# One copy for two carries, the conv gate moved to the head of its slot, and end states scaled on GpSimd

## The chip, the cores and the metric

The kernel runs on one core of one Trainium2 chip. The core has five engines that run their own instruction streams and wait for one another through semaphores: TensorE (PE), VectorE (DVE), ScalarE (ACT), GpSimd (POOL) and SyncE (SP), which issues most transfers here. The metric is the device time in microseconds (us), the median of the runs shown. A trace comes from one profiled execution.

## The reference

A layer in two parts, on x of shape (8, 1024, 256), all in fp32. The first is a selective state-space block, cut here to what matters:

```python
xn = x * rsqrt(mean(x*x) + 1e-6) * norm_w
x_branch, gate = split(xn @ W_in.T)                    # 512 + 512 channels
xc = silu(causal_conv4(x_branch) + conv_b)
dt = soft_clamp(softplus(xc @ W_dt.T + b_dt), 0.001, 0.1, 0.5)
Bp, Cp = xc @ W_B.T, xc @ W_C.T                        # 16 states
dA = exp(soft_clamp(dt[..., None] * A, -8, 8, 0.5))
def step(h, t):
    h = h * dA_t + dB_t * x_t[:, :, None]
    nrm = sqrt(sum(h*h, axis=(1, 2)))                  # over 512 channels x 16 states
    fac = minimum(20.0 / (nrm + 1e-8), 1.0)
    h = where(t % 10 == 0, h * fac, h)
    return h, einsum('bdn,bn->bd', h, C_t) + D_param * x_t
x = layernorm(x + x + scale * ((y * silu(gate)) @ W_out.T))
```

So the state runs freely for ten steps, and then it is scaled down if its norm is above 20. The second part is a mixture of experts (8 experts, top 2) with another layernorm; the change does not touch it.

## The kernel before

`ssm_phase` is the first part and `moe_phase` the second; only the first is changed. The sequence is cut into 52 blocks of 20 steps for all 8 batches. The outer loop over `i` is a pass; a pass has 16 slots `s`. A slot belongs to quarter `q = 4*i + s//4` and to batch `u = s % 4` of that quarter: a quarter is ten time steps of four of the eight batches, one slot is ten steps of one batch. In each slot VectorE runs one `tensor_tensor_scan` (L479) over 128 partitions x 704 elements: 4 channel groups x 16 states x 11 positions, the first of the 11 being the carry, the state with which the ten steps begin. Its factor comes from `DA` (where that first position is 0) and its addend from a PSUM tile `DBX`, one of two halves. In even slots `mult` (L454) writes ten of the 11 positions of two halves and `carry` (L469, or the memset of L464 for the first two quarters) the first one: it takes the last position of the end states `H` of the same four batches, two quarters back, times the factor `FC`. So there are 16 carries of 64 elements in a pass, with a step of 11 elements on either side.

The factor is made once per quarter. ScalarE squares the end states into `SQ` (L285), TensorE sums them over partitions with the constant matrix `ONE` (L703, 1/400), VectorE reduces them to four sums `SN` in slots with u = 2 (`norm_sum`, L485), GpSimd takes the power -0.5 (L631) and bounds it (L633). Behind that, in the same GpSimd slot, it multiplies the states of one batch by C (L640); TensorE then adds up the 16 states with an identity matrix (`y_sum`, L658 and L662).

Each pass also prepares later blocks, two or three ahead, in fixed slots. The queues are in program order, so that order is written out by hand:

- ScalarE: squares of x (L398) in slot 15, `RST` (L294) and `XB` (L301) in slot 1, exponentials of `DA` (L275, 128x2560 elements) in slots 1, 3, 5 and 15, the conv tanh `TB` (L312) in slot 5 behind the exponential, table-changing functions in slot 12, and 64 tanh of `DA` (L383) spread over the slots by the list `DUE`.
- TensorE: the sum of the squares of x (L713) and the projections (L668) in slot 0, conv in slots 2 and 3, the dt products (L687) in slots 6 and 7, which need `XC`.
- VectorE: `XC` (L528) in slot 6 behind that slot's multiplications, carries, `norm_sum` and scan; `dt_x` (L442), the product of dt and x, in slots 0 and 4; `SG` (L557) in slot 15.
- GpSimd: `XN` (L623), the normalized x, in slot 15; it is the input of the next pass's projections.

Of the kernel before, what the change touches and what calls it, by code (L numbers as in the profile page):

```python
# [8 lines left out]
ALU = mybir.AluOpType  # L9
# [9 lines left out]
NQ = 2 * NC  # L19
# [3 lines left out]
def ok(j):  # L23
    return 0 <= j < NB


def ssm_phase(nc, d, YA, X2d, LGd, Bd, Cd):
    ctx = ExitStack()
    with ctx:
# [15 lines left out]
        ID = sb("ID", [128, 128])  # L45
        ONE = sb("ONE", [128, 128])
        MEAN = sb("MEAN", [128, 128])
# [31 lines left out]
        HALF = sb("HALF", [128, 4])  # L79
        FC = sb("FC", [128, 2, 4])  # L80
        PM = ctx.enter_context(nc.psum_tensor("PM", [128, 2048], F32))
        PA = ctx.enter_context(nc.psum_tensor("PA", [128, 512], F32))
# [16 lines left out]
        s_halo, s_sgh, s_dx, s_dxh, s_hc = sem("halo"), sem("sgh"), sem("dx"), sem("dxh"), sem("hc")  # L99
        s_min, s_dt, s_xn, s_pow, s_fac = sem("min"), sem("dt"), sem("xn"), sem("pow"), sem("fac")  # L100
        s_ve, s_sd, s_x2 = sem("ve"), sem("sd"), sem("x2")
# [9 lines left out]

        PRE_C, PRE_CV, PRE_W, N_PRE = 10, 28, 30, 35
        loads = [
# [145 lines left out]
        def scalar_program(eng):  # L259
# [8 lines left out]

            DUE = [0, 0, 3, 8, 13, 15, 18, 26, 34, 36, 41, 48, 55, 55, 55, 59, 64]

# [6 lines left out]
            for i in range(-4, NB + 3):  # L277
                for s in range(16):
                    q = 4 * i + s // 4
                    if s % 4 == 0 and 1 <= q <= NQ - 2:  # L280

                        eng.wait_ge(s_scan, 4 * q)
                        if q >= 2:
                            eng.wait_ge(s_nrm, q - 1)
                        eng.activation(SQ[:], H[:, (q - 1) % 3].rearrange(  # L285
                            "p u (a t) -> p u a t", t=11)[:, :, :, 10], ACT.Square).then_inc(s_hsq, 1)
                    if s == 1 and ok(i + 3):
                        j = i + 3
                        eng.wait_ge(s_ssum, j + 1)
                        if ok(i + 2):  # L290
                            eng.wait_ge(s_br, 2 * j - 1)
                        if j > 0:
                            eng.wait_ge(s_xn, j)
                        eng.activation(RST[:], PA[:, 320:480], ACT.Copy).then_inc(s_ms, 1)  # L294
                    if s == 1 and ok(i + 2):
                        j = i + 2
                        for m, p in enumerate((PA, PZ)):
                            eng.wait_ge(s_br, 2 * j + m + 1)
                            if m == 0 and j > 0:
# [3 lines left out]
                                           ACT.Copy).then_inc(s_xb, 1)  # L303
                    if s in (1, 3, 5) and ok(i):
                        exp_a(i, (s + 1) // 2)
                    if s == 5 and ok(i + 2):
                        j = i + 2
                        for n, (p, m) in enumerate(((PZ, 1), (PA, 0))):
                            eng.wait_ge(s_cv, 2 * j + n + 1)
                            if n == 0 and ok(i + 3):  # L310
                                eng.wait_ge(s_ssum, j + 2)
                            eng.activation(TB[:, 2 * m:2 * m + 2].rearrange("p a b t -> p (a b t)"), p[:, 0:320],  # L312
                                           ACT.Tanh).then_inc(s_th, 1)
                    if s == 9 and ok(i + 2):
                        j = i + 2
# [71 lines left out]
                    if s == 15 and ok(i + 1):  # L387
                        eng.wait_ge(s_z64, 64 * (i + 2))
                        exp_a(i + 1, 0)
                    if s == 15 and ok(i + 4):  # L390

                        j = i + 4
                        eng.wait_ge(s_xt[j % 2], one(j))
                        if ok(i + 1):
                            eng.wait_ge(s_sg, 2 * (i + 2))
                        elif ok(i + 2):
                            eng.wait_ge(s_xc, 2 * (i + 3))
                        eng.activation(TB[:, 0:2].rearrange("p a b t -> p a (b t)"), XT[:, j % 2],  # L398
                                       ACT.Square).then_inc(s_sq, 1)
            lg_out(eng, NB - 1)  # L400
            eng.wait_ge(s_lgd, lg_done(NB))

        def vector_program(eng):
            eng.memset(ONE[:], 1.0 / 400).then_inc(s_pre, 1)
            eng.memset(MEAN[:], 1.0 / 256).then_inc(s_pre, 1)
# [10 lines left out]
            eng.tensor_scalar(PV[:, 0, :], PV[:, 0, :], 0.5, None, ALU.mult).then_inc(s_pre, 1)  # L416
            eng.wait_ge(s_pre, 12)
            for k in range(4):
# [40 lines left out]
            def carry(q, u):  # L459
                o = DBX(u).rearrange("p (a t) -> p a t", t=11)[:, :, 0]  # L460
                if 4 * q + u >= 2:
                    eng.wait_ge(s_scan, 4 * q + u - 1)
                if q < 2:
                    eng.memset(o, 0.0).then_inc(s_ca, 1)  # L464
                else:
                    h = H[:, (q - 2) % 3, u].rearrange("p (a t) -> p a t", t=11)[:, :, 10]
                    if u == 0:
                        eng.wait_ge(s_fac, q - 1)
                    eng.tensor_scalar(o, h, FC[:, q % 2, u:u + 1], None, ALU.mult).then_inc(s_ca, 1)  # L469

            def scan(q, u):
                eng.wait_ge(s_m1, 4 * q + u + 1)
                eng.wait_ge(s_ca, 4 * q + u + 1)
                if u == 0:
# [26 lines left out]
            for i in range(-4, NB + 3):  # L501
                live = ok(i)
                for s in range(16):
# [4 lines left out]
                    if live and s == 4:  # L508
                        dt_x(2 * i + 1)
                    if live and u % 2 == 0:  # L510
                        mult(q, u)
                        mult(q, u + 1)
                        carry(q, u)
                        carry(q, u + 1)
                    if u == 2 and 1 <= q <= NQ - 2:
                        norm_sum(q - 1)
                    if live:
                        scan(q, u)
                    if u == 0 and 0 <= q - 3 < NQ:
                        z_out(q - 3)  # L520
                    if s == 6 and ok(i + 2):
                        j = i + 2
                        for n, (p, m) in enumerate(((PZ, 1), (PA, 0))):
                            eng.wait_ge(s_th, 2 * j + n + 1)
                            if n == 0 and j >= 2:
# [4 lines left out]
                                TB[:, 2 * m:2 * m + 2].rearrange("p a b t -> p (a b t)"), 1.0, p[:, 0:320],  # L530
                                ALU.add, ALU.mult).then_inc(s_xc, 1)
                    if s == 13 and ok(i - 1):
                        j = i - 1
# [34 lines left out]
        def gpsimd_program(eng):  # L568
            eng.wait_ge(s_pre, PRE_CV)
            for i in range(-4, NB + 3):  # L570
                live = ok(i)
                for s in range(16):
# [52 lines left out]
                    if u == 2 and 1 <= q <= NQ - 2:  # L625

                        p = q - 1
                        eng.wait_ge(s_red, p + 1)
                        if p >= 2:
                            eng.wait_ge(s_ca, 4 * (p + 1))  # L630
                        eng.tensor_tensor(FC[:, p % 2], SN[:, p % 2], HALF[:], ALU.pow).then_inc(s_pow, 1)  # L631
                        eng.wait_ge(s_pow, p + 1)
                        eng.tensor_scalar(FC[:, p % 2], FC[:, p % 2], 1.0, 0.0, ALU.min, ALU.max).then_inc(s_fac, 1)  # L633
                    if live:
# [7 lines left out]
        def tensor_program(eng):  # L642
# [49 lines left out]
            for i in range(-4, NB + 3):  # L692
                if i == 0:
                    eng.wait_ge(s_pre, N_PRE)
                for s in range(16):
# [4 lines left out]
                    if u == 0 and 1 <= q <= NQ - 2:  # L700
                        p = q - 1
                        eng.wait_ge(s_hsq, q)
                        eng.matmul(NP(p), ONE[:], SQ[:], start=True, stop=True).then_inc(s_nrm, 1)  # L703
                    if u == 2:
# [556 lines left out]
```

## Time and profile before

| | us |
|---|---|
| median of 3 runs (3082.57 to 3089.11) | 3087.56 |
| the profiled execution, its own time | 3084.8 |
| its span, first to last instruction | 3082.6 |

| engine | busy us | share of the span |
|---|---|---|
| TensorE, matmuls | 2659.4 | 86% |
| VectorE | 2550.2 | 83% |
| ScalarE | 2268.4 | 74% |
| GpSimd | 1993.6 | 65% |

The shares are means over two phases. VectorE is over 90% busy from the second of forty slices of the span to the 33rd and below 40% behind that. The scans start at 77.29 us, the last starts near 2562 and the second phase begins near 2589. A record of VectorE or ScalarE lasts a little longer than the distance to the start of the next one, since the end of one instruction overlaps the start of the next; the time that an instruction occupies is read from start to start. In a timeline the number in brackets is the idle time of the engine ahead of the instruction, with what ended it.

### The profile page before, as it was taken

The page shows a single profiled execution, that of the slowest core. Times are in us where ns is not written, and L with a number is a line of the kernel's source. Part 1 is how long each engine was busy: PE and PEld are TensorE (multiplying, and loading weights), DVE is VectorE, ACT ScalarE, POOL GpSimd, SP SyncE. Part 2 cuts the span into 40 slices and gives each one's busy share as a digit, 9 for nine tenths or more (in the row PEclk, how much of TensorE's full clock was granted, in tenths as well). Part 3 has the DMA queues.
Part 4 walks back from the last instruction along what each step waited for, and adds up shares of the span by engine and source line. Part 5 has one row for each costly group of instructions (what it writes and reads, how often), then busy time and mean ns, then how long its engine had stood idle before and what let it go on. Part 6 is the DMA issues. An engine that isn't in the chain of part 4 may idle for free. (4 is left out here: it accounts for less than half of the span.)

```text
span 3082.6 us, 51144 instructions
## 1 busy us (share of the span) xinstructions
PE 2659.4 (86%) x16400; PEld 2420.8 (79%) x16400; DVE 2550.2 (83%) x3869; ACT 2268.4 (74%) x5161; POOL 1993.6 (65%) x2033
## 2 busy tenths in 40 slices
PE   4899898988989889998899998998999874899992
PEld 4888888888888888888888888888888873667662
DVE  1999999999999999999999999999999996321123
ACT  6888888888888888888888888888888860211113
POOL 0676777777777777777777777777777672443325
PEclk8999999999999999999999999999999986899996
DMA  2122222222222222222222222222222222133226
GB/s 66 57 70 70 71 62 76 70 70 73 66 70 69 70 74 65 72 77 64 72 70 70 70 68 76 68 72 74 63 73 66 69 69 91 31 96 73 73 46 228
DMA packets 153972, 225.69 MB, mean 73 GB/s; under 512 B 46056, under 2 KB 92776, under 8 KB 152552
## 3 DMA queue, kind: packets, MB, share of 16 engines
q1 hardware_dynamic: 131208, 188.98, 21.3%
q0 software_dynamic: 9216, 12.59, 2.3%
q10 hardware_dynamic: 13280, 20.86, 2.0%
q8 instruction: 130, 2.13, 0.3%
q14 instruction: 138, 1.13, 0.1%
HBM read 189.26 MB, written 33.05 MB: 72 GB/s over the span
## 5 line engine op out<-in xcount | busy, mean ns | idle before, releaser
L640 POOL TENSOR_TENSOR H<-H,CB 128x640 f32<-128x640 f32 x832 | 1242.4, 1493 | 499.8 <-DVE H L479 496.6
L479 DVE TENSOR_TENSOR_SCAN H<-DA,PM 128x704 f32<-128x704 f32 x832 | 1322.4, 1605 | 2.5 <-ACT DA L275 2.0
L383 ACT ACTIVATE DA<-DT,SM 128x160 f32<-128x160 f32 x3328 | 1111.7, 430 | 1.3
L662 PE MATMUL YB<-H,ID 128*128 128x160 f32 x6656 | 1052.6, 310 | 0.1
L662 PEld LDWEIGHTS YB<-H,ID 128*128 128x128 f32 x6656 | 991.6, 192 | 16.5 <-issue 11.2
L454 DVE TENSOR_TENSOR PM<-PM,BB 128x640 f32<-128x640 f32 x832 | 640.7, 814 | 5.1 <-issue 0.4
L275 ACT ACTIVATE DA<-DA 128x2560 f32<-128x2560 f32 x208 | 485.4, 2334 | 1.6
L687 PE MATMUL PA<-XC,WDT 128*128 128x160 f32 x832 | 168.3, 371 | 146.9 <-DVE XC L528 146.9
L687 PEld LDWEIGHTS PA<-XC,WDT 128*128 128x128 f32 x832 | 155.2, 246 | 162.5 <-DVE XC L528 162.5
L631 POOL TENSOR_TENSOR FC<-SN,HALF 128x4 f32<-128x4 f32 x206 | 210.5, 1022 | 94.5 <-DVE SN L485 90.5
L1117 POOL DMA_INDIRECT YA<-YS,IG x48 | 75.3, 1569 | 239.6 <-ACT YS L940 228.1
L469 DVE TENSOR_SCALAR PM<-H,FC 128x64 f32<-128x64 f32 x824 | 229.2, 322 | 0.0
L703 PE MATMUL YB<-SQ,ONE 128*128 128x256 f32 x412 | 129.3, 396 | 99.3 <-ACT SQ L285 99.3
L761 PE MATMUL PZ<-WO,Z 128*80 128x256 f32 x832 | 189.8, 381 | 0.1
L1173 PE MATMUL PE<-XTE,W 128*128 128x384 f32 x512 | 169.0, 491 | 10.1 <-issue 9.2
L1183 PE MATMUL PE<-W,HT 128*128 128x256 f32 x768 | 167.7, 380 | 6.1 <-issue 6.1
L1183 PEld LDWEIGHTS PE<-W,HT 128*128 128x128 f32 x768 | 145.3, 190 | 30.2 <-issue 10.7
L761 PEld LDWEIGHTS PZ<-WO,Z 128*80 128x80 f32 x832 | 125.8, 151 | 50.0 <-issue 1.2
L1173 PEld LDWEIGHTS PE<-XTE,W 128*128 128x128 f32 x512 | 97.6, 192 | 78.6 <-issue 13.7
L485 DVE TENSOR_REDUCE SN<-YB 128x4 f32<-128x256 f32 x206 | 85.5, 415 | 85.6 <-PE YB L703 85.6
L703 PEld LDWEIGHTS YB<-SQ,ONE 128*128 128x128 f32 x412 | 65.8, 190 | 112.8 <-ACT SQ L285 112.8
L934 ACT ACTIVATE HT<-PE,B 128x384 f32<-128x384 f32 x64 | 37.1, 582 | 158.0 <-PE PE L1173 155.5
(164 smaller groups left out, 3636.4 us busy)
## 6 DMA issues: line engine op xcount, KB each, us to landing
BB<-Bd SPq DMA_DIRECT2D x208, 320.0 KB, 3.5
CB<-Cd SPq DMA_DIRECT2D x208, 320.0 KB, 3.4
W<-in_w ACTq DMA_DIRECT2D x16, 1024.0 KB
XT<-in_xT SPq DMA_DIRECT2D x52, 160.0 KB, 2.2
XR<-in_xp SPq DMA_DIRECT2D x416, 20.0 KB
X2d<-VV SPq DMA_DIRECT2D x416, 20.0 KB
YA<-VV SPq DMA_DIRECT2D x416, 20.0 KB
HI<-YA SPq DMA_DIRECT2D x6, 1024.0 KB, 10.0
```

The lines of the kernel that those rows point to most:

```text
L275: eng.activation(v, v, ACT.Exp, scale=16.0).then_inc(s_da, 1)
L383: eng.activation(DA[:, c0:c0 + 2, :, a, m, 1:11].rearrange("p c b t -> p b c t"), DT[:, j % 2, a].rearrange("p b (c t) -> p b c t", c=2), ...
L454: eng.tensor_tensor(DBX(u).rearrange("p (a n t) -> p a n t", a=4, n=16)[:, :, :, 1:11], U(c)[:, :, 4 * g + u, :].unsqueeze(2).to_broadcast ...
L469: eng.tensor_scalar(o, h, FC[:, q % 2, u:u + 1], None, ALU.mult).then_inc(s_ca, 1)
L479: eng.tensor_tensor_scan(H[:, q % 3, u], a0, DBX(u), 0.0, ALU.mult, ALU.add).then_inc(s_scan, 1)
L631: eng.tensor_tensor(FC[:, p % 2], SN[:, p % 2], HALF[:], ALU.pow).then_inc(s_pow, 1)
L640: eng.tensor_tensor(h, h, cb, ALU.mult).then_inc(s_hc, 1)
L662: mm = eng.matmul(yv, ID[:], hv[:, :, :, n, 0:10], start=False, stop=n == 15)
L687: mm = eng.matmul(p[:, 160 * a:160 * a + 160], WDT[:, k, c:c + 128], XC[:, j % 2, k].rearrange("p b t -> p (b t)"), start=k == 0, stop=k == 3)
L761: mm = eng.matmul(PZ[0:80, 256 * g:256 * g + 256], zf[:, a, 80 * g:80 * g + 80], WO[:, a, :], start=a == 0, stop=a == 3)
L1173: t = eng.matmul(bank(n)[:, 0:384], W1[:, e % 2, a, 128 * m:128 * m + 128], XT[:, a, 384 * h:384 * h + 384], start=a == 0, stop=a == 1)
L1183: t = eng.matmul(bank(n)[:, 256 * h:256 * h + 256], HT[:, m, 128 * (2 * c + h):128 * (2 * c + h) + 128], W2[:, e % 2, m, :], start=m == 0, ...
```

## The change

Six edits in `ssm_phase`:

- `carry` is called once per pair of slots. It copies 128 elements from a new tile `CAR` into the first positions of both halves of `DBX`. Its waits become the scan of the slot before and `s_car`.
- `CAR`, end states times factor for a whole quarter (128x256 elements), is made by GpSimd behind the factor and ahead of the product with C, in slots with u = 2. It waits for the factor and for the carries of that quarter.
- `ONE` goes; the norm uses `MEAN` (1/256), and the factor is scaled by 1.25 and bounded by 1 in one instruction.
- VectorE's `XC` stands first in slot 6.
- ScalarE's conv tanh stands ahead of the exponential in slot 5.
- ScalarE's squares of x move from slot 15 to slot 0 of the next pass, behind the squares of the end states, and `DUE` spreads the 64 tanh in another way: none in slot 15, three in slot 0.

```diff
-            DUE = [0, 0, 3, 8, 13, 15, 18, 26, 34, 36, 41, 48, 55, 55, 55, 59, 64]
+            DUE = [0, 3, 3, 10, 12, 18, 19, 27, 35, 41, 43, 50, 56, 56, 58, 64, 64]
...
+                    if s == 0 and ok(i + 3):
+                        j = i + 3
+                        eng.wait_ge(s_xt[j % 2], one(j))
+                        if ok(i):
+                            eng.wait_ge(s_sg, 2 * (i + 1))
+                        elif ok(i + 1):
+                            eng.wait_ge(s_xc, 2 * (i + 2))
+                        eng.activation(TB[:, 0:2]..., XT[:, j % 2], ACT.Square).then_inc(s_sq, 1)
...
-                    if s in (1, 3, 5) and ok(i):
-                        exp_a(i, (s + 1) // 2)
                     if s == 5 and ok(i + 2):
                         j = i + 2
...
                             eng.activation(TB[...], p[:, 0:320], ACT.Tanh).then_inc(s_th, 1)
+                    if s in (1, 3, 5) and ok(i):
+                        exp_a(i, (s + 1) // 2)
...
-                    if s == 15 and ok(i + 4):
...
             def carry(q, u):
-                o = DBX(u).rearrange("p (a t) -> p a t", t=11)[:, :, 0]
+                o = PM[:, 640:640 + 2 * CH].rearrange("p (a t) -> p a t", t=11)[:, :, 0]
                 if 4 * q + u >= 2:
-                    eng.wait_ge(s_scan, 4 * q + u - 1)
+                    eng.wait_ge(s_scan, 4 * q + u)
...
-                    h = H[:, (q - 2) % 3, u].rearrange("p (a t) -> p a t", t=11)[:, :, 10]
                     if u == 0:
-                        eng.wait_ge(s_fac, q - 1)
-                    eng.tensor_scalar(o, h, FC[:, q % 2, u:u + 1], None, ALU.mult).then_inc(s_ca, 1)
+                        eng.wait_ge(s_car, q - 1)
+                    eng.tensor_copy(o, CAR[:, u:u + 2].rearrange("p u a -> p (u a)")).then_inc(s_ca, 1)
...
-                    if live and u % 2 == 0:
-                        mult(q, u)
-                        mult(q, u + 1)
-                        carry(q, u)
-                        carry(q, u + 1)
-                    if u == 2 and 1 <= q <= NQ - 2:
-                        norm_sum(q - 1)
-                    if live:
-                        scan(q, u)
-                    if u == 0 and 0 <= q - 3 < NQ:
-                        z_out(q - 3)
                     if s == 6 and ok(i + 2):
                         j = i + 2
...
+                    if live and u % 2 == 0:
+                        mult(q, u)
+                        mult(q, u + 1)
+                        carry(q, u)
+                    if u == 2 and 1 <= q <= NQ - 2:
+                        norm_sum(q - 1)
+                    if live:
+                        scan(q, u)
+                    if u == 0 and 0 <= q - 3 < NQ:
+                        z_out(q - 3)
...
                         eng.wait_ge(s_red, p + 1)
-                        if p >= 2:
-                            eng.wait_ge(s_ca, 4 * (p + 1))
                         eng.tensor_tensor(FC[:, p % 2], SN[:, p % 2], HALF[:], ALU.pow).then_inc(s_pow, 1)
                         eng.wait_ge(s_pow, p + 1)
-                        eng.tensor_scalar(FC[:, p % 2], FC[:, p % 2], 1.0, 0.0, ALU.min, ALU.max).then_inc(s_fac, 1)
+                        eng.tensor_scalar(FC[:, p % 2], FC[:, p % 2], 1.25, 1.0, ALU.mult, ALU.min).then_inc(s_fac, 1)
+                        eng.wait_ge(s_fac, p + 1)
+                        eng.wait_ge(s_ca, 2 * (p + 2))
+                        eng.tensor_tensor(CAR[:], H[:, p % 3].rearrange("p u (a t) -> p u a t", t=11)[:, :, :, 10],
+                                          FC[:, p % 2].unsqueeze(2).to_broadcast([128, 4, 64]),
+                                          ALU.mult).then_inc(s_car, 1)
...
-                        eng.matmul(NP(p), ONE[:], SQ[:], start=True, stop=True).then_inc(s_nrm, 1)
+                        eng.matmul(NP(p), MEAN[:], SQ[:], start=True, stop=True).then_inc(s_nrm, 1)
```

## Rows read from the trace of the kernel before

**Rows 1.** windows of the scan phase: busy us (instructions) of the engines, clock, DMA

```profile
1000.00:1500.00 500.00, 449.57 (x2963) 422.64 (x2962) 481.31 (x711) 435.57 (x998) 365.36 (x375) 0.98 0.26 70
```

**Rows 2.** one line of VectorE: min/median/max ns, first and last start

```profile
L442 DVE TENSOR_TENSOR PM<-DT,XC x104: 481/492/1129, 72.4 to 2530.2; 128x320 f32<-128x320 f32 x104
```

**Rows 3.** waits of the whole run: us in total, times, longest

```profile
PE PA L687 <- DVE XC L528: 146.9, 51, 3.6
...
DVE SN L485 <- PE YB L703: 85.6, 52, 3.7
```

**Rows 4.** timeline of VectorE: start us, us, what, idle before

```profile
1204.57 0.56 DVE L469 TENSOR_SCALAR PM<-H,FC 128x64 f32<-128x64 f32 x2
...
1205.04 1.61 DVE L479 TENSOR_TENSOR_SCAN H<-DA,PM 128x704 f32<-128x704 f32 x1
...
1212.51 0.42 DVE L485 TENSOR_REDUCE SN<-YB 128x4 f32<-128x256 f32 x1 [2.20 <-PE YB L703]
...
1227.99 0.46 DVE L557 SCALAR_TENSOR_TENSOR SG<-TB,PA 128x320 f32<-128x320 f32 x1
...
1245.54 1.53 DVE L454 TENSOR_TENSOR PM<-PM,BB 128x640 f32<-128x640 f32 x2
...
1249.31 0.45 DVE L528 SCALAR_TENSOR_TENSOR XC<-TB,PZ 128x320 f32<-128x320 f32 x1
...
1259.57 0.42 DVE L485 TENSOR_REDUCE SN<-YB 128x4 f32<-128x256 f32 x1 [0.78 <-PE YB L703]
```

**Rows 5.** timeline of TensorE around two waits for XC and one projection

```profile
1201.73 3.85 PE L687 MATMUL PA<-XC,WDT 128*128 128x160 f32 x16 [2.95 <-DVE XC L528]
...
1232.12 1.25 PE L668 MATMUL PA<-XN,WIN 128*128 128x160 f32 x8
...
1250.21 2.44 PE L687 MATMUL PA<-XC,WDT 128*128 128x160 f32 x16 [2.96 <-DVE XC L528]
```

**Rows 6.** timeline of ScalarE

```profile
1199.67 5.55 ACT L383 ACTIVATE DA<-DT,SM 128x160 f32<-128x160 f32 x17
...
1233.45 0.30 ACT L294 ACTIVATE RST<-PA 128x160 f32<-128x160 f32 x1 [2.47 <-issue]
...
1234.83 2.33 ACT L275 ACTIVATE DA<-DA 128x2560 f32<-128x2560 f32 x1
...
1243.44 0.65 ACT L285 ACTIVATE SQ<-H 128x256 f32<-128x256 f32 x1
...
1244.64 2.32 ACT L275 ACTIVATE DA<-DA 128x2560 f32<-128x2560 f32 x1
...
1247.19 0.41 ACT L312 ACTIVATE TB<-PA 128x320 f32<-128x320 f32 x1
```

**Rows 7.** windows behind those two waits; the granted clock is the third last column

```profile
1201.70:1205.40 3.70, 3.67 (x16) 3.67 (x17) 3.70 (x6) 3.70 (x13) 2.54 (x3) 0.60 0.00 0
...
1250.20:1253.90 3.70, 3.69 (x26) 3.69 (x27) 3.70 (x6) 3.70 (x12) 2.54 (x3) 1.00 0.00 0
```

**Rows 8.** page, one line and timeline: carries, their memsets, a copy

```profile
L469 DVE TENSOR_SCALAR PM<-H,FC 128x64 f32<-128x64 f32 x824 | 229.2, 322 | 0.0
...
L464 DVE MEMSET PM<- x8: 112/112/112, 75.1 to 91.9; 128x64 f32 x8
...
2594.22 0.29 DVE L964 COPY PE<-MC 128x128 f32<-128x128 f32 x1
```

**Rows 9.** lines of GpSimd: min/median/max ns, first and last start

```profile
L580 POOL TENSOR_TENSOR DX<-XC,SM x52: 1248/1257/1268, 40.9 to 2489.7; 128x640 f32<-128x640 f32 x52
...
L623 POOL TENSOR_TENSOR XN<-XT,RST x52: 859/1120/1133, 14.1 to 2423.2; 128x320 f32<-128x320 f32 x52
...
L640 POOL TENSOR_TENSOR H<-H,CB x832: 1462/1481/1742, 79.1 to 2563.5; 128x640 f32<-128x640 f32 x167
```

**Rows 10.** timeline of GpSimd at the end of a pass

```profile
1226.22 1.02 POOL L631 TENSOR_TENSOR FC<-SN,HALF 128x4 f32<-128x4 f32 x1
...
1228.95 1.11 POOL L623 TENSOR_TENSOR XN<-XT,RST 128x320 f32<-128x320 f32 x1
```

More of the change, by code:

```diff
@@ L45, in ssm_phase @@
         ID = sb("ID", [128, 128])
-        ONE = sb("ONE", [128, 128])
         MEAN = sb("MEAN", [128, 128])
@@ L80, in ssm_phase @@
         FC = sb("FC", [128, 2, 4])
+        CAR = sb("CAR", [128, 4, 64])
         PM = ctx.enter_context(nc.psum_tensor("PM", [128, 2048], F32))
@@ L99, in ssm_phase @@
         s_halo, s_sgh, s_dx, s_dxh, s_hc = sem("halo"), sem("sgh"), sem("dx"), sem("dxh"), sem("hc")
-        s_min, s_dt, s_xn, s_pow, s_fac = sem("min"), sem("dt"), sem("xn"), sem("pow"), sem("fac")
+        s_min, s_dt, s_xn, s_pow, s_fac, s_car = (
+            sem("min"), sem("dt"), sem("xn"), sem("pow"), sem("fac"), sem("car"))
         s_ve, s_sd, s_x2 = sem("ve"), sem("sd"), sem("x2")
@@ L110, in ssm_phase @@
         KD = 0.5 / (0.0495 + 1e-8)
-        PRE_C, PRE_CV, PRE_W, N_PRE = 10, 28, 30, 35
+        PRE_C, PRE_CV, PRE_W, N_PRE = 9, 27, 29, 34
         loads = [
@@ L286, in scalar_program @@
                             "p u (a t) -> p u a t", t=11)[:, :, :, 10], ACT.Square).then_inc(s_hsq, 1)
+                    if s == 0 and ok(i + 3):
[5 more added lines that the diff above has]
+                            eng.wait_ge(s_xc, 2 * (i + 2))
+                        eng.activation(TB[:, 0:2].rearrange("p a b t -> p a (b t)"), XT[:, j % 2],
+                                       ACT.Square).then_inc(s_sq, 1)
                     if s == 1 and ok(i + 3):
@@ L389, in scalar_program @@
                         exp_a(i + 1, 0)
-                    if s == 15 and ok(i + 4):
[L392 to L399, printed above, removed]
             lg_out(eng, NB - 1)
@@ L403, in vector_program @@
         def vector_program(eng):
-            eng.memset(ONE[:], 1.0 / 400).then_inc(s_pre, 1)
             eng.memset(MEAN[:], 1.0 / 256).then_inc(s_pre, 1)
@@ L416, in vector_program @@
             eng.tensor_scalar(PV[:, 0, :], PV[:, 0, :], 0.5, None, ALU.mult).then_inc(s_pre, 1)
-            eng.wait_ge(s_pre, 12)
+            eng.wait_ge(s_pre, 11)
             for k in range(4):
@@ L465, in carry @@
                 else:
-                    h = H[:, (q - 2) % 3, u].rearrange("p (a t) -> p a t", t=11)[:, :, 10]
                     if u == 0:
-                        eng.wait_ge(s_fac, q - 1)
-                    eng.tensor_scalar(o, h, FC[:, q % 2, u:u + 1], None, ALU.mult).then_inc(s_ca, 1)
+                        eng.wait_ge(s_car, q - 1)
+                    eng.tensor_copy(o, CAR[:, u:u + 2].rearrange("p u a -> p (u a)")).then_inc(s_ca, 1)
             def scan(q, u):
                 eng.wait_ge(s_m1, 4 * q + u + 1)
-                eng.wait_ge(s_ca, 4 * q + u + 1)
+                eng.wait_ge(s_ca, 2 * q + u // 2 + 1)
                 if u == 0:
```

## The prediction

> **What bounds the kernel now.** I read the windows first [rows 1]. In the 500 us from 1000 on, VectorE is busy 481.3 us, TensorE 449.6, ScalarE 435.6 and GpSimd 365.4, so VectorE sets the pace of the scan phase and the others have some room. A pass of the loop over i is 16 slots and computes 20 time steps. Its two products dt·x (slots 0 and 4) start from 72.4 to 2530.2 us, 104 of them, which is 51.25 passes: 47.96 us each [rows 2]. In a pass TensorE works 43.1 us of that, ScalarE 41.8 and GpSimd 35.0 (the busy times over 500, times 47.96).
>
> The waits of the whole run [rows 3] show the one thing for which VectorE stands still: the reduction of the norms, 85.6 us in 52 waits, one in each pass, for TensorE's L703. So a pass is 46.3 us of work and 1.65 us of waiting. The timeline of VectorE [rows 4] places the wait: 2.20 us ahead of the reduction at 1212.51 and 0.78 in the pass behind (1259.57). It is the reduction in slot 10, and the reader is to ask why TensorE is late there. The same list says it: TensorE itself waits 146.9 us for XC, 2.8 us in each pass. Before it goes on at 1250.21 it has stood since 1247.25 [rows 5]. XC could not come sooner, as VectorE has the slot's multiplications, carries, reduction and a scan (from 1245.54) ahead of it, XC starting at 1249.31 [rows 4], and ScalarE runs an exponential (1244.64) ahead of the two tanh that XC needs, the last of them until 1247.6 [rows 6]. The wait costs TensorE more than its length: its 16 matmuls behind one such wait took 3.85 us at a granted clock of 0.60, behind the next 2.44 us at 1.00 [rows 5, 7]. That is the lower of its two levels, 1.2 GHz, in a part of the passes and the full 2.4 in the others, and 1.41 us between them; 2.20 less 0.78 is 1.42. By the Trainium skill ("TensorE: Matmul & The Clock Gate", the part on the HAM clock gate) an array that idles falls to the lower level; the trace agrees in every other pass.
>
> **The change, part by part.** I call T0 the end of a pass's last scan, which is the start of SG at 1227.99 [rows 4], and count from it.
>
> *Carries.* Removed: 824 tensor_scalar of 64 elements, 322 ns each [rows 8]. Records overlap, so I take starts: a pair begins at 1204.57 and the scan behind it at 1205.04, 0.47 us [rows 4]. Added: one copy of 128 elements from SBUF to PSUM for each pair. The trace has a copy of just that size and direction: 289 ns [rows 8]. A record of this engine outlasts the start of the next by about 0.08 us (a pair of 0.56 takes 0.47), so it occupies 0.21 us. The gain is 0.26 us for each of 412 pairs (the first two quarters of the sequence have memsets): 107 us, or 2.1 us in a pass. The row's target is contiguous and ours has a step of 11 elements. The memsets with that same target took 112 ns for 64 elements [rows 8], so the step is cheap on the write side, and I put the old carry's slowness down to reading H with that step, or to its pointer factor. If it were the writing, 128 elements would cost 156 + 2x167 = 490 ns (289 less 133 of streaming is 156; 323 less 156 is 167), 0.41 us occupied, and the gain 0.06x412 = 25 us. The copy is nearest to its twin row: 107, with 25 as far end.
>
> *XC first and the conv tanh ahead of the exponential.* VectorE's XC comes up 3.7 us sooner in the pass, at the start of slot 6. No work is removed by it. ScalarE's tanh pair comes 2.23 us sooner (one exponential of 2.32, less an overlap of 0.09). TensorE then goes from its running sum almost straight into the dt products: its wait of 3 us is nearly gone, and with it the slow stretch. What VectorE waited for is done 3.0 us sooner, 4.4 where the clock was down, against 2.20 and 0.78; VectorE comes to that reduction only 0.8 sooner (three carry pairs). So the 85.6 us go, and I keep 4 of them for the first passes, where TensorE's lateness has other reasons: 82 us.
>
> *Squares, and the table of tanh dates.* The squares of x go from slot 15 to slot 0 of the next pass, behind the squares of the states; 64 tanh remain 64. TensorE has its input for the norm 0.4 us sooner and that for the mean of x² later. RST then waits for the projection that stands behind both in TensorE's queue, now with 3 tanh to fill the 2.47 us that ScalarE idles there [rows 6]. No cost for VectorE as long as ScalarE keeps up, seen below.
>
> *GpSimd.* Four products CAR of 128x256 in a pass, each with one more semaphore step. The trace has no such product. The nearest row below is 1257 ns for 640 elements with a factor that is constant along the row; by size that is 0.50 us for 256. The nearest above is 1.12 us for two full streams of 320 elements [rows 9]. H is read with a step here, which speaks for a time above the middle of 0.8, the fewer elements for one below; I take 0.8. GpSimd goes to 38.2 us a pass, room left. Queued behind CAR are the products H·C of slots 2, 6, 10, 14 and, in slot 15, XN; the carries wait for it.
> The new wait: the reduction in slot 2 releases pow (1.02), the minimum and CAR, together 2.3 us. The carry of slot 4 comes 4.9 us behind the reduction (two scans, dt·x, two multiplications). Where GpSimd comes late to pow, as in slot 14 at 1226.22, the factor is there at 1227.5 (XN's start at 1228.95 less one product with C) [rows 10]; CAR ends at 1228.4, T0+0.7 with T0 itself 0.27 sooner by a carry pair, and the carry of slot 0 starts at T0+2.9. By the same count the room is 2.6 in slot 4, 2.2 in slot 8 and 2.1 in slot 12. So CAR may cost up to 3.0, 3.4, 3.0 and 2.9 us in the four places before a carry waits, and it is hidden at either bound.
> XN ended at 1230.06 and moves to T0+3.2; the projection started at 1232.12, T0+4.1 [rows 5, 10]. TensorE could now come to it at T0+1.9, so it will wait 1 us there. RST starts 1.2 later, at T0+4.4, and the tanh pair is done after 1.38 + 2 exponentials (4.46) + 15 tanh (0.32 each by 17 in 5.43, 4.8) + the squares (0.56) + 0.8, that is T0+16.4 (it was T0+19.6) [rows 6]. VectorE wants the first of them at T0+16.8 (XC at T0+21.3 now, less 3.77 for slot 6, less three carry pairs). The cover is thin, 0.4 us.
> The norm of slot 10: TensorE starts the dt products 15.1 us behind the projection (1232.12 to 1247.2), at T0+18.2, and 9.4 us later the norm is there (1250.21 to 1259.57), T0+27.6. VectorE was ready for it at T0+30.8 (1259.57 less 0.78, less 1227.99) and will be at 29.2, six pairs sooner: 1.6 us of room [rows 4, 5].
> Removing ONE, the factor 1.25 and the single bound swap constants and cost nothing; the carry's stronger wait for the scan before is one that the second multiplication makes anyway. The load of CB waits for H·C and moves back by CAR, and lands some 5 us ahead of its use.
>
> *Is another engine next?* VectorE's work becomes 46.3 - 2.1 = 44.2 us. TensorE's, at full clock, is 43.1 - 0.7 = 42.4; in the walk it idles 1 us for XN and 0.7 at T0. ScalarE's is 41.8, with 1.5 to 2 us of idling around RST, 43.7. Both stay under 44.2, ScalarE by half a microsecond.
>
> **Sum.** The profiled execution took 3084.8 us. 3084.8 - 107 - 82 = 2895.8. The median shown, 3087.6, is 2.8 above it, so 2898.6: I say 2899. The phase behind the scan is untouched.
>
> **Rivals.**
> 1. *ScalarE or the tanh pair becomes the bound.* With cover of 0.4 us, a CAR of 1.12 or a later squaring makes VectorE wait for XC, now with all of slot 6 behind it. At 1 us a pass: 52 us, 2951. For it: the margins above. Against: ScalarE is idle for 6 us of a pass today and can give up four of them.
> 2. *The wait for the norms stays.* TensorE is the next engine by its own load; if its new idle places (XN, T0) push it so that L703 comes late again, only the carries gain: 3087.6 - 107 = 2981. Against: it has the 1.6 us of room at slot 10.
> 3. *The copy is as slow as the carries*, 25 in place of 107: 2981 too.
> 4. *SBUF contention.* dt·x, which reads two SBUF tensors, takes 492 ns in the middle and 1129 at worst, and XN 859 at least and 1120 in the middle [rows 2, 9]: the two slow one another when they meet. More GpSimd work means more such meetings; all 104 at the worst would give back 66 us: 2965. The Trainium skill ("Perfetto Trace Analysis", on optimizing Scalar/DVE operations) warns that moving work between VectorE and GpSimd might not help, since they share an SBUF read port. The scan's rows, 1.61 us whether or not GpSimd works, show none of it.
> 5. *Slower.* The carry's new wait for CAR takes the place of the old. It decides from CAR = 4.0 us: beyond 12.3 us for four of them (the sum of the four rooms) VectorE waits in full, and what the change saves is 3.7 us a pass. At 5 us a CAR it would wait 7.7, 4.0 more than saved: 3087.6 + 208 = 3296. For it: pow takes 1.02 us for 4 elements on this engine, so that its time is not always that of the size. Against: the products with C take 1.48 us for 640 elements and at most 1.74 [rows 9].
> That it does not do what it says is covered by 2.
>
> **Chances.** Forecast 0.72, rival 1 0.11, rival 2 0.05, rival 3 0.04, rival 4 0.03, slower 0.04, and 0.01 for no change. The forecast's own range is 2885 (the copy at 0.20 and all waits gone) to 2925. To hold 8 in 10 it is drawn to 2950, nearly all of rival 1. A difference of 0.2%, 6 us, is about what can be told from no change. Faster by more 0.95, within 0.01, slower 0.04.
>
> **What would show it.** Right: the carry group at 412 copies of about 290 ns; L703 gone from VectorE's waits; L687's wait for XC below 0.7 us a pass and no window at a low granted clock in the scan phase; dt·x from start to start of a pass 44.2 us; CAR near 0.8 us. Wrong: a wait of VectorE at XC for the tanh (rival 1), at the copy for CAR (rival 5), at L485 again (rival 2), or a copy of nearly 490 ns (rival 3). A pass above 45 us with no wait of VectorE would say that its own instructions grew (rival 4).

## The result: faster by 3.9%, and 67 us short of the forecast

| | before | after |
|---|---|---|
| median, us (4 runs each) | 3085.76 | 2965.55 |
| lowest to highest | 3082.57 to 3089.11 | 2959.9 to 2971.9 |
| ratio of after to before, 95% interval | | 0.9611 [0.9588, 0.9634] |

The direction was right. The size was not: 2899 was forecast, with a range up to 2950. The profiled execution of the kernel after took 2959.9 us, its span is 2958.1.

First the windows of the kernel after, the columns as in [rows 1]:

```profile
1000.00:1500.00 500.00, 472.85 (x3114) 437.21 (x3114) 493.05 (x660) 456.61 (x1041) 422.51 (x440) 0.99 0.27 74
```

VectorE is now busy 493 of 500 us (481 in [rows 1]), so it waits less, and TensorE's granted clock is 0.99 in place of 0.98. The waits of the whole run answer to [rows 3]:

```profile
ACT RST L305 <- PE PA L670: 134.3, 49, 3.7
...
PE PA L670 <- POOL XN L622: 57.0, 48, 1.7
...
DVE XC L517 <- ACT TB L321: 38.3, 15, 22.7
...
PE PA L689 <- DVE XC L517: 2.1, 2, 1.0
```

VectorE's wait for the norms, 85.6 us before, has no row any more, and TensorE's wait for XC, 146.9 us before, is down to 2.1. TensorE waits for XN, 57 us or 1.2 a pass. VectorE's wait for the tanh at XC is 38.3 us in all, most of it at the start of the kernel, as before (32.4 in 4 waits); in the stretch from 100 to 2400 us it is 4.2 us.

So the waits went as forecast. What grew stands in the groups of VectorE, shapes kept apart, and in one group of GpSimd:

```profile
L469 DVE COPY PM<-CAR 128x128 f32<-128x128 f32 x412 | 116.4, 283 | 0.0
L442 DVE TENSOR_TENSOR PM<-DT,XC 128x320 f32<-128x320 f32 x104 | 87.3, 839 | 0.0
...
L633 POOL TENSOR_TENSOR CAR<-H,FC 128x256 f32<-128x256 f32 x206 | 155.3, 754 | 17.3
```

The copy takes 283 ns, as its twin row said (289), and CAR 754 (0.8 forecast). But dt·x, an instruction that the change does not touch, takes 839 ns in the mean and 87.3 us in all. The same group of the kernel before:

```profile
L442 DVE TENSOR_TENSOR PM<-DT,XC 128x320 f32<-128x320 f32 x104 | 52.3, 503 | 0.0
```

That is 35 us more. The timeline of VectorE in one pass shows it, and a second thing:

```profile
1213.34 0.48 DVE L442 TENSOR_TENSOR PM<-DT,XC 128x320 f32<-128x320 f32 x1
...
1215.39 0.28 DVE L469 COPY PM<-CAR 128x128 f32<-128x128 f32 x1
1215.76 1.62 DVE L479 TENSOR_TENSOR_SCAN H<-DA,PM 128x704 f32<-128x704 f32 x1
...
1220.49 0.28 DVE L469 COPY PM<-CAR 128x128 f32<-128x128 f32 x1
1220.68 0.41 DVE L485 TENSOR_REDUCE SN<-YB 128x4 f32<-128x256 f32 x1
...
1224.05 1.11 DVE L442 TENSOR_TENSOR PM<-DT,XC 128x320 f32<-128x320 f32 x1
1225.07 1.55 DVE L454 TENSOR_TENSOR PM<-PM,BB 128x640 f32<-128x640 f32 x2
```

dt·x takes 0.48 us in slot 0 and 1.11 in slot 4. The whole trace has the same: that of slot 4 is held up in 51 of 52 passes, that of slot 0 in 6. And a copy occupies 0.19 us where the reduction follows (1220.49 to 1220.68), but 0.37 us where the scan follows (1215.39 to 1215.76), and so it is for the 206 of each kind. The sum had 0.21 for both.

### The profile page after: what moved, and what is told of

It reads as the page before. It is cut to its first block and busy times, and to the rows that moved or that the text cites. A ratio compares the mean times of both kernels' runs of the same rounds, so it can differ in the third digit from the quotient of the medians.

```text
span 2958.1 us, 50935 instructions
## 1 busy us (share of the span) xinstructions
PE 2648.4 (90%) x16400; PEld 2381.6 (81%) x16400; DVE 2488.2 (84%) x3452; ACT 2265.4 (77%) x5161; POOL 2165.0 (73%) x2239
## 3 DMA queue, kind: packets, MB, share of 16 engines
q14 instruction: 135, 1.11, 0.1%
## 5 line engine op out<-in xcount | busy, mean ns | idle before, releaser
L642 POOL TENSOR_TENSOR H<-H,CB 128x640 f32<-128x640 f32 x832 | 1262.9, 1526 | 273.9 <-DVE H L479 268.3
L670 PE MATMUL PA<-XN,WIN 128*128 128x160 f32 x832 | 153.8, 332 | 58.5 <-POOL XN L622 57.0
L670 PEld LDWEIGHTS PA<-XN,WIN 128*128 128x128 f32 x832 | 129.2, 208 | 70.8 <-POOL XN L622 68.7
L633 POOL TENSOR_TENSOR CAR<-H,FC 128x256 f32<-128x256 f32 x206 | 155.3, 754 | 17.3
L670 PE MATMUL PZ<-XN,WIN 128*128 128x160 f32 x832 | 140.0, 313 | 27.5 <-DVE VV L539 27.5
L705 PE MATMUL YB<-SQ,MEAN 128*128 128x256 f32 x412 | 128.2, 393 | 38.4 <-ACT SQ L286 38.4
L670 PEld LDWEIGHTS PZ<-XN,WIN 128*128 128x128 f32 x832 | 124.8, 200 | 37.2 <-DVE VV L539 37.2
```

Source lines behind the costliest of these rows:

```text
L633: eng.tensor_tensor(CAR[:], H[:, p % 3].rearrange("p u (a t) -> p u a t", t=11)[:, :, :, 10], FC[:, p % 2].unsqueeze(2).to_broadcast([128, ...
L642: eng.tensor_tensor(h, h, cb, ALU.mult).then_inc(s_hc, 1)
L670: mm = eng.matmul(p[:, 160 * a:160 * a + 160], WIN[:, k, c0 + 128 * a:c0 + 128 * a + 128], XN[:, j % 2, k], start=k == 0, stop=k == 1)
```

## The experiments

Each kernel was timed against the kernel before on its own chip. The ratios to the kernel before are comparable among them; the kernel after stands at 0.9611.

| kernel | us | ratio, 95% interval | dt·x in all, us |
|---|---|---|---|
| after | 2965.6 | 0.9611 [0.9588, 0.9634] | 87.3 |
| e1, copies and CAR alone | 3101.7 | 1.0064 [1.0045, 1.0083] | 84.3 |
| e2, orders alone | 3000.6 | 0.9725 [0.9708, 0.9741] | 59.0 |
| e3, copy between the multiplications | 2935.3 | 0.9507 [0.9492, 0.9523] | 108.3 |
| e4, dt·x ahead of the scan | 2954.0 | 0.9574 [0.9558, 0.9590] | 113.0 |
| e6, dt·x behind the scan | 2912.4 | 0.9445 [0.9429, 0.9461] | 49 |
| e7, e6 and e3 together | 2872.8 | 0.9313 [0.9298, 0.9329] | 49.0 |
| e8, XC behind the scan again | 3112.3 | 1.0092 [1.0075, 1.0109] | 97.2 |
| e9, exponential ahead of tanh again | 3043.2 | 0.9867 [0.9851, 0.9884] | 125.9 |
| e10, dt·x with one SBUF input | 2920.9 | 0.9465 [0.9449, 0.9480] | 49.8 |

The theory behind them: 35 us of the shortfall come from dt·x meeting a GpSimd product that CAR has pushed back, and 33 us from the scan's wait for the whole copy. The rivals: the order of the work is to blame; the copy's strided PSUM target is; dt·x is slow for another reason of its place.

### e1 and e2: the two halves of the change

e1 is the kernel before with this alone (and MEAN for ONE):

```diff
-                        carry(q, u)
-                        carry(q, u + 1)
+                        carry(q, u)          # one copy from CAR, as in the change
...
+                        eng.tensor_tensor(CAR[:], H[:, p % 3]..., FC[:, p % 2]..., ALU.mult).then_inc(s_car, 1)
```

> The kernel before with the carry part alone: CAR on GpSimd, one copy for two carries, MEAN for ONE; every order as before. My theory: the copy itself is as cheap as forecast (about 0.28 us), but it is followed by a scan that now waits for the whole of it in the four slots of a pass that have no norm reduction in between (0.37 us from copy to scan, against 0.47 for a pair of carries), and dt.x of slot 4 takes 1.1 us in place of 0.49 since CAR delays GpSimd's product with C into it. Per pass: 4 x 0.10 + 4 x 0.28 = 1.5 us gained, 0.63 lost in dt.x, and 0.38 given back at slot 10, where VectorE arrives sooner at a norm that comes no sooner: 0.5 us a pass, 26 us, about 3060 us. The forecast's own step (107 us with nothing given back) would give 2979. A rival that puts the shortfall on the order of the work expects 2979 too, with dt.x at 0.49.

Measured: 3101.7 us, slower than before by 0.6%, where a gain of 26 us was expected. The waits of e1 at the norm and at XC, and its dt·x with the columns of [rows 2]:

```profile
PE PA L689 <- DVE XC L527: 126.3, 51, 3.3
...
DVE SN L485 <- PE YB L705: 116.9, 51, 4.2
```

```profile
L442 DVE TENSOR_TENSOR PM<-DT,XC x104: 485/998/1422, 71.8 to 2520.1; 128x320 f32<-128x320 f32 x104
```

The profiled execution took 3074.4 us, 10 less than that of before. That nearly adds up: the copies save 1.5 us a pass by the starts above (four times 0.47 less 0.37, four times 0.47 less 0.19), 78 us; dt·x costs 84.3 - 52.3 = 32 more; the wait for the norms grows from 85.6 to 116.9, 31; that leaves 15. VectorE saves time and hands it back at slot 10, where it waits for TensorE, which waits for VectorE's XC. TensorE is slow there more often, too: by its timeline the 16 matmuls behind the wait for XC take 3.8 us or more in 36 of 51 passes of e1, against 27 of 51 before, and 2.44 in the others. The other executions of e1 took 3097 to 3113 us; what they spent more is not in this trace and stays open. What holds either way: without the new order the copies gain at most 10 of the 78 us that they save.

e2 is the other half:

```diff
                     if live and u % 2 == 0:
                         mult(q, u)
                         mult(q, u + 1)
                         carry(q, u)
+                        carry(q, u + 1)      # tensor_scalar from H and FC, as before; no CAR
```

> The kernel after with the carries, their waits and the factor's bound wait as before (no CAR, no copy): XC first, conv tanh ahead of the exponential, squares and tanh dates as in the change. My theory: the 85 us of waits at the norm go and nothing else changes, since without CAR the products with C stay where they were and dt.x stays at 0.49 us: about 3003 us, no window at a low TensorE clock in the scan phase. A rival that puts the shortfall on the order (XC in the way, a new wait for the tanh) expects 3040 to 3070, with VectorE waiting at XC or dt.x at 1.1 us here too.

Measured: 3000.6 us against 3003. No wait for the norm, granted clock 1.00 in the window from 1000 to 1500 us, a pass of 46.34 us nearly all through. The rival that blames the order falls: the order is worth 85 us by itself. The dt·x of e2:

```profile
L442 DVE TENSOR_TENSOR PM<-DT,XC x104: 481/508/1137, 70.8 to 2446.8; 128x320 f32<-128x320 f32 x104
```

Without CAR that of slot 4 stays at 0.49. That of slot 0 takes 0.63 in most passes, which was not expected and costs 7 us in all; it meets the tail of a GpSimd product (e4 shows what that does). The halves are worth -16 and 85 us apart and 120 together.

### e3: the wait from copy to scan

```diff
                         mult(q, u)
-                        mult(q, u + 1)
                         carry(q, u)
+                        mult(q, u + 1)
```

> The kernel after with the copy between the two multiplications of its slot, not behind them. The scan then waits for a copy that is long done. My theory: the 0.16 to 0.18 us from the end of the copy to the scan in four slots of a pass go, 0.65 us a pass, 34 us: 2932 us, ratio to the kernel after 0.989; dt.x in slot 4 stays at 1.1 us. Rival: the time belongs to the copy itself or to its strided PSUM target, so moving it changes nothing: 2965. Second rival: GpSimd's CAR is wanted 0.73 us sooner and VectorE waits for it at the copy: slower than 2965.

Measured: 2935.3 us, 30 less than after, against 34 expected. In the timeline of VectorE the copy occupies 0.19 us and nothing is left between the second multiplication and the scan:

```profile
1037.89 0.28 DVE L469 COPY PM<-CAR 128x128 f32<-128x128 f32 x1
1038.08 0.82 DVE L454 TENSOR_TENSOR PM<-PM,BB 128x640 f32<-128x640 f32 x1
1038.81 1.60 DVE L479 TENSOR_TENSOR_SCAN H<-DA,PM 128x704 f32<-128x704 f32 x1
```

So the time belonged to the wait and not to the copy or its target. It is in the code: before, the scan of the first half waited for the first of its two carries and the second ran meanwhile; now there is one copy and the scan waits for the end of it. CAR is wanted sooner by one multiplication, and no wait for it appears. At the same time dt·x grew from 87.3 to 108.3 us, so the wait by itself was worth more than 30; by the starts it is 206 times 0.18, 37 us.

### e4, e6 and e10: what dt·x waits for

e4 puts dt·x where GpSimd seemed to be idle:

```diff
-                    if live and s == 0:
-                        dt_x(2 * i)
-                    if live and s == 4:
-                        dt_x(2 * i + 1)
...
                         carry(q, u)
+                    if live and s == 4:
+                        dt_x(2 * i + 1)
+                    if live and s == 12 and ok(i + 1):
+                        dt_x(2 * i + 2)
```

> The kernel after with the two dt.x products of a pass put between the copy and the scan of slots 4 and 12 (the one for the next pass's first half comes four slots early), where GpSimd has finished its products with C and waits for a scan. My theory (the two engines hold one another up at SBUF when dt.x, with two SBUF inputs, meets a GpSimd product): every dt.x at 0.49 us, which gives 0.63 us a pass, and the wait from copy to scan is hidden in these two slots, 0.33 us: 0.96 us a pass, 50 us, about 2916 us. Rival (dt.x is slow for its operands or its PSUM target, or because of what VectorE ran before it): dt.x of slot 4 stays at 1.1 us, and only 0.33 us a pass is gained, 2948. In both, VectorE may wait up to 0.3 us a pass at XC for the tanh, since it comes sooner to it.

Measured: 2954.0 us. Neither figure: dt·x takes 0.91 us in slot 4 and 1.29 in slot 12. The premise was wrong, since GpSimd's second product still runs there, and this is what made the cause readable. VectorE and GpSimd in slot 4 of e4, and in slot 12:

```profile
1222.84 0.91 DVE L442 TENSOR_TENSOR PM<-DT,XC 128x320 f32<-128x320 f32 x1
1223.66 1.61 DVE L479 TENSOR_TENSOR_SCAN H<-DA,PM 128x704 f32<-128x704 f32 x1
...
1244.47 1.29 DVE L442 TENSOR_TENSOR PM<-DT,XC 128x320 f32<-128x320 f32 x1
```

```profile
1220.47 2.92 POOL L645 TENSOR_TENSOR H<-H,CB 128x640 f32<-128x640 f32 x2
...
1242.50 2.91 POOL L645 TENSOR_TENSOR H<-H,CB 128x640 f32<-128x640 f32 x2
```

The two GpSimd products end at 1223.39 and 1245.41, and dt·x ends at 1223.75 and 1245.76: 0.36 and 0.35 us behind, however long it has been there. A third case, in e3, is a dt·x of 1.63 us from 1024.47 to 1026.10, beside a product from 1024.27 to 1025.74, 0.36 again.

These are not picked. In the traces of all kernels here 498 dt·x take 0.58 us or more, and every one ends 0.35 to 0.36 us behind the end of a GpSimd product that began before it. dt·x does not run slowly. It stands until the GpSimd instruction is over and then runs its 320 elements.

e6 puts it straight behind the first scan of slots 4 and 12, for whose end GpSimd's next product waits and starts 0.2 us later:

```diff
                     if live:
                         scan(q, u)
+                    if live and s == 4:
+                        dt_x(2 * i + 1)
+                    if live and s == 12 and ok(i + 1):
+                        dt_x(2 * i + 2)
```

> The kernel after with the two dt.x products of a pass straight behind the first scan of slots 4 and 12. In the run before this one dt.x ended 0.36 us behind the end of GpSimd's product whenever it had met one, however early it started. My theory is thus a lock: dt.x does not begin before the running GpSimd product is over. Behind that scan GpSimd is idle and starts 0.2 us later than VectorE, so dt.x comes first: every dt.x at 0.49 us (36 us less in all than in the kernel after), and the 0.17 us from dt.x to the multiplication of slot 0 go, 9 us: about 2921 us. Rival (dt.x is slow in slot 4 for its operands or for what TensorE writes to PSUM then): dt.x stays at 0.9 to 1.1 us, and about 2955.

Measured: 2912.4 us, 9 better than expected. All 104 are short now:

```profile
L442 DVE TENSOR_TENSOR PM<-DT,XC x104: 473/473/493, 71.2 to 2361.7; 128x320 f32<-128x320 f32 x104
```

e10 leaves dt·x in its place, where it meets the product, and changes one operand. It leaves x out of the product, so its states are other numbers; shapes and counts are the same, and only its time is of use:

```diff
-                eng.tensor_tensor(U(c), DT[:, j % 2, :, :, t], XC[:, j % 2, :, :, t], ALU.mult)
+                eng.tensor_tensor(U(c), DT[:, j % 2, :, :, t], U(c - 1), ALU.mult)    # PSUM
```

> The kernel after with every instruction in its place, but dt.x multiplies dt with the last U, which lies in PSUM, in place of xc, so that it has one SBUF input and not two. It leaves x out of the product, and the states are others; shapes and counts are the same. Theory (GpSimd's product holds up only a VectorE instruction that reads two SBUF tensors): all dt.x at about 0.49 us, 36 us less in all than in the kernel after, about 2930 us. Rival (any VectorE instruction with a strided SBUF input is held up, or dt.x is slow in slot 4 for its place alone): dt.x of slot 4 stays at 1.1 us and the time at 2965.

Measured: 2920.9 us against 2930 expected and 2965 by the rival:

```profile
L446 DVE TENSOR_TENSOR PM<-DT,PM x102: 471/480/488, 119.7 to 2368.5; 128x320 f32<-128x320 f32 x102
```

It has 471 to 488 ns everywhere, in slot 4 too. So the place is not it, nor a strided SBUF input, since dt is read as before: it is the second SBUF input. The Trainium skill says so ("GPSIMD Engine Reference", Key points): GpSimd shares its SBUF interfaces with VectorE and contends with instructions that have two SBUF inputs. The runs agree: here dt·x waits for all that is left of the GpSimd instruction, and with one SBUF input it does not wait.

### e7: both causes away

e7 has the edits of e6 and e3.

> The same with the copy between the two multiplications as well, so that both named causes of the shortfall are taken away. Theory: all dt.x at 0.49 us and no wait from copy to scan, a pass of 43.9 to 44.2 us: 2870 us if nothing else comes up. VectorE then comes to XC at 16.5 us behind the end of the last pass, with the tanh pair there at about 16.9, so it may wait there 0.3 to 0.5 us a pass: up to 2895. Rival: a third cause stands behind the two (ScalarE as the bound), and the time stays above 2910.

Measured: 2872.8 us, 3.1% below the kernel after, and the fastest of all. The window of e7:

```profile
1000.00:1500.00 500.00, 484.12 (x3244) 453.75 (x3245) 498.33 (x684) 471.31 (x1076) 431.01 (x456) 1.00 0.29 78
```

Its passes take 43.78 us, nearly all of them, and VectorE is busy 498.3 of 500 us. No wait of 0.3 us a pass for the tanh appeared, only one of 2.4 us between 100 and 2400. The gain over after adds up from the starts: dt·x 87.3 - 49.0 = 38 us, the copies 37, and 9 where the multiplication of slot 0 no longer waits for the dt·x just ahead of it; that is 84, and the two profiled executions are 87 apart. So without its two side effects the change would not stand at 2873: the 9 us, and copies of 0.19 us in all places, come from the moves of e6 and e3. It would stand near the forecast of 2899 (2965.6 less 29 and 35 is 2902).

### e8 and e9: is each half of the new order needed?

e8 puts VectorE's XC back behind the scan of slot 6 in the kernel after, e9 puts ScalarE's exponential back ahead of the conv tanh:

```diff
# e8, VectorE
-                    if s == 6 and ok(i + 2):      # XC, ahead of mult, carry, norm_sum, scan
...
+                    if s == 6 and ok(i + 2):      # XC, behind them
```

```diff
# e9, ScalarE
+                    if s in (1, 3, 5) and ok(i):
+                        exp_a(i, (s + 1) // 2)
                     if s == 5 and ok(i + 2):      # conv tanh
...
-                    if s in (1, 3, 5) and ok(i):
-                        exp_a(i, (s + 1) // 2)
```

> The kernel after with XC back behind the scan of slot 6 and all else as after: it undoes the order of VectorE alone. Theory: XC's place is what removed the waits for the norms. TensorE stands at its dt products for some 3 us again, and VectorE waits at the reduction of slot 10 for 1.0 us a pass at the full clock and 2.5 where the clock has fallen: 3020 to 3090 us, with windows at a low granted clock. Rival (the earlier tanh and squares did it, XC's place did nothing): at most 2980, no wait at the reduction.

> The kernel after with the exponential of slot 5 ahead of the conv tanh again. Theory: with XC first in its slot the tanh has to be early. It ends 2.2 us later, and VectorE waits at XC about 1.1 us in each pass: 57 us, about 3022 us, with no wait at the norm. Rival (ScalarE has room enough, the order there did nothing): 2965, and no wait at XC.

e8 took 3112.3 us, above its span of 3020 to 3090. The wait for the norms is back and larger than ever, and in the pass around 1205.9 us TensorE's granted clock behind its wait for XC is 0.59, against 0.60 and 1.00 in [rows 7]:

```profile
PE PA L689 <- DVE XC L527: 162.4, 51, 3.6
...
DVE SN L485 <- PE YB L705: 145.2, 50, 4.2
```

```profile
1205.90:1209.70 3.80, 3.77 (x16) 3.77 (x17) 3.71 (x5) 3.80 (x12) 3.64 (x4) 0.59 0.01 3
```

A kernel with copies, CAR, early tanh and the new dates, but XC in its old place, is 0.9% slower than the one before: the XC edit alone is worth 147 us in this company. Against the kernel before, the wait for the norms costs 60 us more and dt·x 45 (97.2 less 52.3), and the copies save 78: 27 of the 28 us. TensorE's 16 matmuls behind the wait take over 3.7 us in 44 of 51 passes.

e9 took 3043.2, 78 us above after; 57 were expected. Its wait for the tanh and its dt·x:

```profile
DVE XC L517 <- ACT TB L323: 76.4, 31, 22.6
```

```profile
L442 DVE TENSOR_TENSOR PM<-DT,XC x104: 485/1114/1645, 71.1 to 2485.5; 128x320 f32<-128x320 f32 x104
```

The wait grew by 38 us, less than expected, and dt·x by 39 (125.9 against 87.3), 77 of the 78. A wait at XC shifts VectorE against GpSimd, and dt·x of slot 0 then meets a product from its start more often: it takes over 1 us in 38 of 52 passes, against 4 in the kernel after. So here too the rival falls, the early tanh is needed, and the miss has the same cause as that of the forecast.

## Why the prediction missed, step by step

- **The bound and the wait for the norms: right.** XC late, TensorE idle, clock down, L703 late: e2 takes the chain away and gains 85 us, with 82 in the sum; e8 and e9 show that both edits are needed.
- **The copy: duration right, what it occupies wrong.** The sum took 0.21 us for all 412, from the overlap of two records. That overlap is there only if the next instruction does not wait for this one. It holds for the 206 copies with a reduction behind (0.19) and fails for the 206 with a scan (0.37): 206 x 0.16 less 206 x 0.02 is 29 us. The step that failed is "so it occupies 0.21 us" (measured: 0.19 and 0.37), and behind it the sentence on the stronger wait, which looked at what the copy waits for and not at what the scan waits for. That used to be the first of two carries. The far end of 25 us was for another reason (a strided target), and e3 shows it was not that. The price of such a wait could be read in the trace of before, on dt·x: the multiplication of slot 0 waits for the dt·x just ahead of it, that of slot 4 does not, and dt·x occupies 0.58 us in the first and 0.41 in the second.

```profile
1228.85 0.49 DVE L442 TENSOR_TENSOR PM<-DT,XC 128x320 f32<-128x320 f32 x1
1229.43 1.56 DVE L454 TENSOR_TENSOR PM<-PM,BB 128x640 f32<-128x640 f32 x2
...
1239.92 0.50 DVE L442 TENSOR_TENSOR PM<-DT,XC 128x320 f32<-128x320 f32 x1
1240.33 1.55 DVE L454 TENSOR_TENSOR PM<-PM,BB 128x640 f32<-128x640 f32 x2
```

- **GpSimd: CAR's price right, what it pushes priced too low.** 0.75 us against 0.8, and no wait of a carry for it. The prediction did list the products behind CAR, but only asked who waits for their results. It did not ask with which VectorE instruction they now run side by side. In the pass of [rows 4] dt·x of slot 4 started at 1239.92, and GpSimd's product of slot 2, started at 1238.58, was over at about 1240.06 (a product takes 1.48): dt·x slipped in between two products. With CAR ahead of them they run 0.75 us later, and dt·x finds one in its middle, in 51 of 52 passes: +0.63 us a pass. GpSimd there, before and after:

```profile
1238.58 3.18 POOL L640 TENSOR_TENSOR H<-H,CB 128x640 f32<-128x640 f32 x2 [0.23 <-DVE H L479]
```

```profile
1222.61 0.75 POOL L633 TENSOR_TENSOR CAR<-H,FC 128x256 f32<-128x256 f32 x1
1223.31 3.17 POOL L642 TENSOR_TENSOR H<-H,CB 128x640 f32<-128x640 f32 x2
```

So the step that failed is that the forecast put what CAR pushes at nothing; measured, it is 35 us (87.3 less 52.3). Rival 4 named the mechanism, from the two rows of dt·x and XN, but it got 3 in 100, because "More GpSimd work means more such meetings" was left as a matter of chance. It was not one: a walk of slot 4 of the same kind as was made for the carries gives it. Its sign, a pass above 45 us with no wait of VectorE, is what was seen, but for the 4 us at the tanh. That its worst case also says 2965 is luck: it has 66 us for all 104 dt·x, and the shortfall is 35 from half of them and 29 from the copies.
- **Rival 1**, the thin cover at the tanh, cost 4.2 us from 100 to 2400 us. TensorE's wait for XN, put at 1 us, is 1.2.
- **The sum again:** 2899 + 29 + 35 + 4 = 2967, against 2965.6. By the profiled executions, and with none of the 85.6 us of waits kept, it is 2895.8 - 3.6 + 29 + 35 + 4 = 2960.2, against 2959.9. Passes of 45.6 us (104 starts of dt·x from 71.3 to 2407.2, over 51.25) stand against the 44.2 forecast.
- **Range and chances.** The top of 2950 came from rival 1 at 1 us a pass. With rival 4 at a chance such as the walk gives it, it would have reached to 2965.

## What to carry to other kernels

An instruction that is delayed on an engine off the critical path changes not only when its result is there, but also what it runs beside; walk its new neighbours, above all VectorE instructions with two SBUF tensors beside GpSimd. What an instruction occupies depends on whether the next one waits for it, so take the price from a place with the same wait, and put another instruction in between where that is free. And cheaper work on an engine that stands still once a pass for another one gains little or nothing until that wait is gone: the copies alone gave -16 us, the order alone 85, and both 120.

## What the runs showed of the hardware

dt·x, a VectorE instruction with two SBUF inputs, and a GpSimd product of two SBUF tensors exclude one another for the whole instruction. dt·x ended 0.35 to 0.36 us behind the product in all 498 cases, at lengths of 0.58 to 1.64 us; with one input in PSUM it took 0.48 us in the same place. It works the other way round too, as this row of GpSimd in the kernel after shows, the product that meets the dt·x of 1213.34 and takes 2.00 us where 1.48 is its median [rows 9]:

```profile
1213.15 2.00 POOL L642 TENSOR_TENSOR H<-H,CB 128x640 f32<-128x640 f32 x1
```

That product's record begins 0.19 us ahead of dt·x, and yet dt·x ran first. In the traces here dt·x went first in all 75 cases in which the product's record began less than 0.19 us before it, and waited in all 427 in which the product had begun more than 0.21 us before and ran on for at least 0.2 us; between the two, 93 went first and 69 waited. The dt·x of e3 above, 0.20 us behind, waited. So a shift of some hundredths of a microsecond decides over more than 1 us of VectorE, and it explains why dt·x of slot 0 is long in some passes and short in others.

Whether a scan or a copy with one SBUF input is ever held up: none of the traces shows it (no scan of this size takes over 1.62 us in any of them). Not tried was what made the old carries of 64 elements slow, 322 ns against 283 for a copy of 128; both the step of H and the pointer factor remain possible.
